# ScalarE's order in the lead of a state-space scan: where the dt weights are split, where the exponentials of the sums are taken, and which load a wait counts

## The reference

```
x = x + L0_attn(layernorm(x))     # linear attention, 8 heads used
x = x + L0_ffn(layernorm(x))      # base weight + top-2 of 8 low-rank experts
x = x + L1_attn(layernorm(x))     # the state-space block, below
x = x + L1_ffn(layernorm(x))      # base weight + top-1 of 4 low-rank experts
```

```
proj = h @ in_proj_w.T                       # gate, hBC, dt
hBC  = silu(causal_conv4(hBC) + conv_b)      # x, B, C
dt   = softplus(dt + dt_bias);  A = -exp(A_log)
A_cumsum = cumsum(A * dt)                    # in each chunk: "the sums"
L = exp(segment_sum(A * dt))                 # decay inside a chunk
Y = (C B^T * L) @ (x * dt)  +  (C @ states) * exp(A_cumsum) + D * x
out = (rmsnorm(Y) * norm_w * silu(gate)) @ out_proj_w.T
```

## Time and profile before

| | |
|---|---|
| time, 3 runs | median 1794.5 us (1792.48 to 1795.0) |
| the profiled execution | 1794.74 us, span 1793.2 us |
| busy: PE / DVE / ACT / POOL | 1686.6 / 1196.7 / 1267.4 / 727.2 us |
| mean granted TensorE clock | 0.974 |
| the state-space block's norm and lead | about 213 to 320 us |
| its groups 0 to 7 | about 320 to 1700 us |

### The profile page before, as it was taken

One profiled execution on the slowest core, in us unless ns is written; L12 is line 12 of the kernel. 1 busy time (PEld: TensorE's weight loads), 2 busy tenths in 40 slices (PEclk: granted clock), 3 DMA queues, 4 the chain that ended last, 5 costly groups with the idle time before them and its releaser, 6 DMA issues. The chain is left out here.

```text
span 1793.2 us, 26687 instructions
## 1 busy us (share of the span) xinstructions
PE 1686.6 (94%) x9420; PEld 1377.3 (77%) x9420; DVE 1196.7 (67%) x1847; ACT 1267.4 (71%) x2165; POOL 727.2 (41%) x786
## 2 busy tenths in 40 slices
PE   5998687999999999999999999999999999999839
PEld 4776476788888888888888888888888888888637
DVE  4565576766776677667766776677667766776853
ACT  3332145987798779877987798779877987798611
POOL 2543112444344434543454345434543454344620
PEclk9998898999999999999999999999999999999959
DMA  4220124323232323232323232323232323232121
GB/s 153 97 86 1 66 68 131 113 91 107 83 113 91 108 83 113 91 108 83 112 90 108 83 113 90 109 83 112 90 109 83 111 92 108 83 111 69 53 74 48
DMA packets 99428, 166.46 MB, mean 93 GB/s; under 512 B 11712, under 2 KB 49984, under 8 KB 97888
## 3 DMA queue, kind: packets, MB, share of 16 engines
q1 hardware_dynamic: 99296, 164.75, 28.5%
HBM read 158.43 MB, written 6.29 MB: 92 GB/s over the span
## 5 line engine op out<-in xcount | busy, mean ns | idle before, releaser
L217 PE MATMUL bank<-xh,w_h 128*128 128x512 f32 x1152 | 462.9, 402 | 11.7 <-DVE m_xc L1271 9.8
L218 PE MATMUL bank<-xl,w_h 128*128 128x512 f32 x1152 | 450.7, 391 | 0.0
L219 PE MATMUL bank<-xh,w_l 128*128 128x512 f32 x1152 | 449.8, 390 | 0.0
L1069 POOL TENSOR_TENSOR m_z_l<-m_zg,m_z_h 128x512 fp32r<-128x512 f32 x128 | 178.0, 1391 | 574.5 <-ACT m_z_h L1193 574.5
L1123 ACT ACTIVATE m_mt<-m_mt,m_unit 128x128 f32<-128x128 f32 x1024 | 312.1, 390 | 0.0
L1048 POOL TENSOR_TENSOR w_l<-w_raw,w_h 128x512 fp32r<-128x512 f32 x144 | 186.2, 1293 | 244.7 <-ACT w_h L1090 244.7
L1282 DVE TENSOR_TENSOR x<-x,bank 128x512 f32<-128x512 f32 x128 | 87.9, 687 | 274.3 <-PE bank L219 274.3
L217 PEld LDWEIGHTS bank<-xh,w_h 128*128 128x128 f32 x1152 | 217.1, 188 | 64.9 <-issue 22.0
L1271 DVE SCALAR_TENSOR_TENSOR m_xc<-bank,m_par_conv,m_xc 128x1020 f32<-128x1020 f32 (+2 forms) x192 | 244.6, 1274 | 15.0 <-ACT m_xc L1102 10.0
L219 PEld LDWEIGHTS bank<-xh,w_l 128*128 128x128 f32 x1152 | 216.9, 188 | 46.3
L218 PEld LDWEIGHTS bank<-xl,w_h 128*128 128x128 f32 x1152 | 217.3, 189 | 41.0
(11 more groups left out here) (238 smaller groups left out, 2768.3 us busy)
## 6 DMA issues: line engine op xcount, KB each, us to landing
m_mt<-ncs_rows SPq DMA_DIRECT2D x128, 512.0 KB, 3.8
w_raw<-w_in SPq DMA_DIRECT2D x144, 256.0 KB, 3.1
m_wo_raw<-w_out_in SPq DMA_DIRECT2D x64, 256.0 KB, 5.1
m_e<-ecs_rows SPq DMA_DIRECT2D x128, 128.0 KB, 3.4
a_wo_raw<-wo_in SPq DMA_DIRECT2D x8, 1024.0 KB, 5.0
x<-x_in SPq DMA_DIRECT2D x8, 256.0 KB, 4.6
a_wq_raw<-wq_in SPq DMA_DIRECT2D x8, 256.0 KB, 4.0
e_wb_raw<-f_base SPq DMA_DIRECT2D x2, 1024.0 KB, 7.7
```

Source lines behind the costliest of these rows:

```text
L217: nc.tensor.matmul(out, ah, bh, start=first, stop=False)
L218: nc.tensor.matmul(out, ah, bl, start=False, stop=False)
L219: return nc.tensor.matmul(out, al, bh, start=False, stop=last)
L1069: nc.gpsimd.tensor_tensor(z_l[:, s % 2, :, :], zg[:], f(z_h[:, s % 2, :, :]), ALU.subtract).then_inc(zl_ready, 1)
```

## The change

Three things are altered, all inside `ssm_block`.

1. The loads of `dt_bias` and `a_log` count on a semaphore of their own, `bias_loaded`. ACT waits for `w_dt` alone before it splits the dt weights, and for the other two where it first reads them.
2. The three splits that ACT ran ahead of the norm's evictions (`dt_h` and the tiles 8 and 9 of `w_h`) now stand behind the evictions of tiles 1, 3 and 5.
3. ACT's exponentials of the sums, and with them SP's store of `ecs` and its loads of the rows, stand one step later.

```
@@ sync @@
             sp.dma_start(dt_raw, w_dt.rearrange("p k h -> p (k h)")).then_inc(dt_loaded, 16)
             for m in range(LEAD, LEAD + W_BUFS):
                 load_tile(-1, m)
-            sp.dma_start(bias[:], dt_bias).then_inc(dt_loaded, 16)
-            sp.dma_start(alog[:], a_log).then_inc(dt_loaded, 16)
+            sp.dma_start(bias[:], dt_bias).then_inc(bias_loaded, 16)
+            sp.dma_start(alog[:], a_log).then_inc(bias_loaded, 16)
...
                     sp.dma_start(ncs_dram.rearrange("t h s -> h t s"),
                                  ncs.rearrange("p (t s) -> p t s", t=NT)).then_inc(ncs_stored, 16)
-                    sp.wait_ge(exps_ready, 1)
-                    sp.dma_start(ecs_dram, ecs[:].rearrange("p a b -> p (a b)")).then_inc(ecs_stored, 16)
+                if s == 13:
                     sp.wait_ge(ncs_stored, 16)
                     for row in range(ROW_BUFS):
                         load_rows(0, row)
                 if s == 14:
+                    sp.wait_ge(exps_ready, 1)
+                    sp.dma_start(ecs_dram, ecs[:].rearrange("p a b -> p (a b)")).then_inc(ecs_stored, 16)
                     sp.wait_ge(packed_ready, 3)
@@ scalar @@
-            def weights_high():
-                act.wait_ge(dt_loaded, 48)
-                nc.scalar.activation(dt_h, dt_raw.rearrange("p (k h) -> p k h", k=KT), ACT.Copy).then_inc(dt_hi, 1)
-                w_high(-1, LEAD)
-                w_high(-1, LEAD + 1)
-
-            norm_scalar(nc, act, n, xh, weights_high)
+            def weights_high(t):
+                if t == 1:
+                    act.wait_ge(dt_loaded, 16)
+                    nc.scalar.activation(dt_h, dt_raw.rearrange("p (k h) -> p k h", k=KT), ACT.Copy).then_inc(dt_hi, 1)
+                if t in (3, 5):
+                    w_high(-1, LEAD + t // 4)
+
+            norm_scalar(nc, act, n, xh, after=weights_high)
 
             def prepare(s):
                 if s == NT:
+                    act.wait_ge(bias_loaded, 32)
                     nc.scalar.activation(a_pos[:], alog[:], ACT.Exp).then_inc(a_ready, 1)
...
-                if s == 12:
+                if s == 13:
                     act.wait_ge(ncs_ready, 1)
```

More of the change, by code:

```diff
@@ L777, in ssm_block @@
     dt_loaded = sem("dt_loaded")
+    bias_loaded = sem("bias_loaded")
     dt_hi = sem("dt_hi")
```

## The result

The changed kernel takes 1790.13 us (median of 8 runs, 1788.26 to 1790.68) beside 1794.75 us for the kernel before (8 runs, 1792.48 to 1797.65): ratio 0.9971, 95% interval 0.9963 to 0.9980. A second measurement (e5) gave 1790.04 beside 1794.22, ratio 0.9979 (0.9970 to 0.9987). So it is faster, by 4.2 to 4.6 us where the forecast was 7.7, and the time lies 0.3 us inside the upper end of the range. It lies above the forecast's own range (1785.3 to 1788.3) and 0.5 us above the top of rival 1 (1789.6), in the strip that was added for spread. The profiled execution took 1790.04, span 1788.5, mean granted clock 0.974 as before.

The account below looks back on a forecast made before the run. The prediction took a chain hopping between engines in the norm and lead, 213 to 320 us, as the bound. Terms -5.1 (norm) and -2.6 (exponentials) made -7.7 from 1794.74: 1787.0 us, range 1784.6 to 1790.4.

Parts of the forecast that it names:

- rival 1: At the sums, exponentials in series hold TensorE, so their move brings only 0 to 1.2 us; 1788.4 to 1789.6, chance 0.15.
- The first term, -5.1: In the norm, ScalarE's first eviction and the dt products come about 5.1 us earlier; bounds -6.4 to -2.8.
- I cost them at nothing: In the norm, three splits of 0.53 us fit into ScalarE's idle time between evictions; without that cover 1.6 us.
- The second term, -2.6: At the sums, moving the exponentials one step later turns `end` 2.6 us earlier; bounds nothing to -2.9.
- TensorE's new wait: Ahead of the transposes of the sums, TensorE would wait about 1.0 us for `exps_ready`.
- The eviction of tile 12 is done long before: At the sums, VectorE's taps of tile 12 need not wait for ScalarE's eviction and start 2.93 us earlier.
- The drain: A skill rule at ScalarE's table load: 1.38 us more per switch, leaving the exponentials' move 1.2 us; the prediction rejected it.
- No wait there can swallow time won earlier.: From 320 to 1550 us TensorE is always busy at full clock, so earlier gains carry through.
- rival 2: In the norm, the clock rises late or splits delay evictions; gain there 2.8 to 4.0 us, 1788.1 to 1789.3, chance 0.10.
- rival 3: In the norm, a split waits for its late load, holding evictions; gain there about 0.5 us, 1791.6, chance 0.08.
- rival 4: The rows of the sums, loaded about 5 us later, land too late for `decay`; slower, 1798.3 us, chance 0.04.

Follow-up runs that it names:

- e5: The changed kernel measured a second time, unaltered: 1790.04 us, ratio 0.9979 against the kernel before.
- e7: Kernel before with only the separate semaphore, so ScalarE waits for the dt weights alone, splits still ahead of the evictions: 1792.99 us, ratio 0.9996.
- e10: Kernel before with only the splits moved between the evictions, the dt split still waiting for all three loads: 1789.41 us, ratio 0.9971.
- e4: Changed kernel with GpSimd's low part of weight tile 14 held until the sums are ready: 1788.22 us, ratio 0.9971 against the kernel before.
- the filled pair: Changed kernel and kernel before, each with nine unread TensorE products added ahead of group 0: 1786.79 and 1792.63 us.
- e2: Kernel before with only the exponentials moved one step later, norm as before: 1794.95 us, ratio 1.0003.
- e1: Kernel before with only the norm's part, own semaphore and splits between the evictions, exponentials as before: 1790.51 us, ratio 0.9981.
- e8: Changed kernel plus nine unread products before group 0, GpSimd's tile 14 split held, and sums' transposes released by the sums: 1786.78 us, ratio 0.9960.
- e12: Changed kernel with TensorE's transposes of the sums released by the sums, the wait for the exponentials moved behind them: 1789.14 us, ratio 0.9966.

## Why the prediction was right, and where it was off

*The first term, -5.1.* Right in its mechanism and, between the two first profiles, in its size (-4.98, evictions 5.09 earlier from the root). "I cost them at nothing" held for the splits: after the first of them ScalarE still waits 0.46 to 0.78 us for TensorE ahead of the evictions of tiles 2 to 5, and from the third tile's turning to `dt_half(0)` it took 4.75 us where it was 4.62. That the size fitted so well was luck in the pair. What I took from one profile varies. The first eviction came 6.98 to 8.33 us behind the root in the five profiles with the old norm, since the load of `a_log` lands sooner or later (4.6 us after its issue in the first profile of before, 4.3 in the changed kernel's, 3.1 in e7's and e10's), and the clock's rise moved `dt_half(1)` on top of that, by up to 0.8 us among the profiles of the new norm and up to 1.5 among those of the old. The five profiles with the old norm have 19.55 to 21.64 from root to dt, mean 20.63; the seven with the full new one 16.09 to 16.86, mean 16.60. The term is -4.0 on average. The forecast didn't say how much of it the separate wait brings and how much the place of the splits; e10 and e7 show that the place is what counts.

*The second term, -2.6.* Its pieces came as written: VectorE straight from `neg_last` to the taps, TensorE's new wait (1.45 for 1.0), `exps_ready` bound by ScalarE's own chain. (The sum for `exps_ready` gives 291.03, not 291.05, which changes nothing.) From the sums to the decay it is 24.62 or 24.63 us in the six profiles with the new order and no early turning, and 26.09 to 27.35, mean 26.87, in the six with the old: -2.2 on average. The old order had TensorE's tile 14, at half clock for a time that varies, on the path. In e7's profile the clock was back at full 10.4 us behind `neg_last` and the stretch took 26.09; in the first profile of before it was 13.2 us, and 27.35. In the new order ScalarE's exponentials cover that, and the 24.62 don't vary. The step that failed is a clause: "The eviction of tile 12 is done long before". So it was, and with it the split of tile 14, and GpSimd's part of it now fell on VectorE's chain ahead of `neg_last`. I had counted it as time to spare on ScalarE and had not asked what it runs beside. It cost 0.94 to 0.98 in every profile with the new order and without e4's wait. The part is thus worth 1.3 on the chain, half of what was forecast.

The page "GPSIMD Engine Reference" of the Trainium skill, section "1. Specifications", says that GpSimd shares its SBUF interfaces with VectorE, with contention when VectorE has two SBUF inputs. The instruction that went from 1.23 to 2.19 us has two, and so has the one of 2.20 us in the kernel before; both rows and e4 agree with the rule.

*The drain.* The rule of the Trainium skill's page "ScalarE: Activation LUTs", section "What ACT_TABLE_LOAD costs", that the prediction weighed would put 1.38 us of drain beside the table load. The silu ahead of the load ends at 284.42, the load at 284.44 lasts 1.28 us, and the exponential starts at 285.73, 1.29 behind the load's start. The trace doesn't agree with the rule, and going by the row was right.

*"No wait there can swallow time won earlier."* This was said of the groups from 320 us on, and the sum carried the gain through the entry to group 0 unchanged. That step failed. The clock fell at or just behind TensorE's two pauses there in seven of ten profiles without filling, and each fall cost 1.4 to 2.9 us. In the first profile of before it hadn't fallen, and I read the stretch as fixed. The rival that put the clock in doubt looked only at the norm.

With these sizes the change is worth -4.0 + 1.0 - 2.2 = -5.2 us up to the first decay, and the filled pair measured -5.6, which is as near as its intervals allow to tell. Without the filling the medians gave -4.6 and -4.2. The missing microsecond points at the entry: filling gained 2.6 to 3.1 us on the changed kernel and 1.6 on the one before. Whether the fall really is more frequent or dearer behind the change, or these two numbers differ by chance (their intervals overlap), is open: two profiles of each kernel don't tell. On e2 filling gained 4.8 us, though the entries of the ten unfilled profiles are only 1.2 us longer on average than the filled ones. So the profiles don't account for the whole gain of the filling either.

That the time fell within the range was luck too. The range reached up to 1790.4 for a weak second part (rival 1), a late clock in the norm (rival 2) and some spread. The overlap with GpSimd and the fall of the clock at the entry stood nowhere in it, and without the room for the others the time would have been outside.

*The rivals.* That the second part brings little (0 to 1.2 us, rival 1) came nearly true with 1.3 on the chain, by another way than the exponentials in the open. The late clock in the norm (rival 2) is seen in e1, e4, e5, e8 and e12, 0.7 us, not the 1.1 to 2.3 that the rival needs. A load that takes over the wait (rival 3) is seen in e10 and e7, at 0.5 us each. The rows of the sums (rival 4) never mattered: issued from 281.74 on, they landed 3.8 to 7.8 us after their issue, so by 291.0, and ScalarE wanted them at 297.86, where it went from the preceding split straight on. The changed kernel's timeline of SP's queue (start of issue, time that issuing took):

```profile
281.74 1.85 SPq L953 DMA_DIRECT2D m_mt<-ncs_rows  x4
...
290.98 0.43 SPq L994 DMA_DIRECT2D ecs_rows<-m_y  x1
```

## What to carry to other kernels

A wait that a single instruction needs should not stand ahead of work that doesn't need it. Moving that instruction behind the first pieces of the stream took 5.2 us off (e10); relaxing its wait in place took 1.2, which its interval doesn't tell from nothing (e7). When an engine's work is moved earlier, ask also which engine then runs beside which: a hidden split cost VectorE's chain nearly a microsecond, and the trace of before had a row that showed it. A gain on a chain of hand-offs can be partly lost at a later place where TensorE pauses and its clock may fall; here nine unused products in such a pause brought 1.6 to 4.8 us. And a size taken from one profile of each kernel can be off by a microsecond: take a second before trusting a term of that size.

## What the hardware showed that I had not expected

The granted clock fell at or within 1.1 us behind a pair of pauses of 2.2 and 0.8 us with only four short transposes between, in some executions and not in others of the same program (before 8.68 and 10.29), and was back at full 3.4 us later, in one profile 6.8: a stretch of 8.7 us took 10.1 to 11.6. With nine unused products of 512 columns (2.20 us) in the first pause it stayed up in all four profiles that had them, against three of ten without, and the changed kernel was 2.6 to 3.1 us faster. A VectorE instruction with two SBUF inputs of 128 x 1024 took 2.19 us for 1.23 beside a GpSimd subtraction of 128 x 512 that itself took 1.30, no longer than alone; one tile earlier, where GpSimd started first by 0.55 us and behind another such instruction, VectorE's took 2.20 and GpSimd's 1.67. And a load of half a kilobyte took 3.1 us to land in one execution and 4.6 in another.
